# Cross attention on one Trainium2 core: the reads of the stacked low key halves are issued from ScalarE's queue

## The reference

```
x = x + tanh(g_xattn) * attention(layernorm(x), ctx, ctx)    # 16 heads of 16, q from x, k and v from ctx
x = x + tanh(g_ffn)   * ffn(layernorm(x))                    # gated experts into v, attention, gated experts out

# cross attention, 32 batches, 100 queries, 361 keys, width 256
scores = (q @ k.T) / sqrt(16);  scores = where(mask, scores, min);  attn = softmax(scores)
O = (attn @ v) @ Wo.T + bo
```

## Time and profile before

| | |
|---|---|
| median of 3 runs | 2054.14 us (2052.46 to 2054.36) |
| the profiled execution: time | 2055.4 us |
| the profiled execution: span | 2053.6 us |
| busy in the span | PE 93%, DVE 73%, ACT 56%, POOL 45% |
| issues of line 405 | 256 of 90.2 KB, median 4.9 us from issue to landing |

### The profile page before, as it was taken

One profiled execution on the slowest core, in us unless ns is written; L12 is line 12 of the kernel. 1 busy time (PEld: TensorE's weight loads), 2 busy tenths in 40 slices (PEclk: granted clock), 3 DMA queues, 4 the chain that ended last, 5 costly groups with the idle time before them and its releaser, 6 DMA issues. The chain is left out here.

```text
span 2053.6 us, 59326 instructions
## 1 busy us (share of the span) xinstructions
PE 1916.2 (93%) x13454; PEld 1163.7 (57%) x13454; DVE 1497.0 (73%) x4285; ACT 1143.3 (56%) x3588; POOL 933.5 (45%) x1361
## 2 busy tenths in 40 slices
PE   5698999999988799999999999968999999999998
PEld 2477777777777555544444444436555555555553
DVE  6477777777777796255555555555999999999989
ACT  3477777777777644444444444434555555555543
POOL 3011121122111200266666666653766666777767
PEclk9899999999999899999999999987999999999999
DMA  3666665676666158300000000025222222222201
GB/s 115 114 106 97 103 108 99 104 102 105 106 101 89 51 223 322 128 26 26 26 26 26 26 26 26 26 91 165 79 73 76 72 76 72 76 75 70 84 14 64
DMA packets 192129, 173.99 MB, mean 85 GB/s; under 512 B 51921, under 2 KB 183378, under 8 KB 190034
## 3 DMA queue, kind: packets, MB, share of 16 engines
q1 hardware_dynamic: 189906, 165.06, 34.5%
q0 software_dynamic: 2176, 8.39, 1.2%
HBM read 112.41 MB, written 60.98 MB: 84 GB/s over the span
## 5 line engine op out<-in xcount | busy, mean ns | idle before, releaser
L1315 POOL TENSOR_TENSOR o_side<-o_side,o_tmp 128x256 f32 (+1 forms) x528 | 397.7, 753 | 192.2 <-POOL o_side L1315 73.2
L593 ACT ACTIVATE c_ex<-c_sm,c_nmax 100x361 f32<-100x361 f32 x512 | 303.9, 594 | 157.7 <-DVE c_nmax L486 136.5
L1041 ACT ACTIVATE big<-e_pv,gates 128x128 f32<-128x128 f32 x800 | 228.7, 368 | 291.4 <-PE e_pv L1103 290.1
L486 DVE CUSTOM_DVE_ANT_0 c_sm<-c_ps,c_mbias 100x361 f32<-100x361 f32 x512 | 270.3, 528 | 137.7 <-PE c_ps L665 135.8
L1436 ACT ACTIVATE o_tmp<-o_py,gates 128x256 f32<-128x256 f32 x528 | 222.3, 474 | 190.6 <-PE o_py L1509 140.8
L1103 PE MATMUL e_pv<-e_vhi,e_xhi 128*128 x800 | 303.2, 379 | 1.2 <-ACT e_out L1031 1.2
L1509 PE MATMUL o_py<-o_whi,a_chi 128*128 128x512 f16 x800 | 303.9, 380 | 0.1
L979 DVE TENSOR_SCALAR e_acc<-e_pv,gates 128x128 f32<-128x128 f32 x400 | 122.0, 347 | 249.1 <-PE e_pv L1103 249.1
L1103 PE MATMUL e_pv<-e_vlo,e_xhi 128*128 x800 | 303.2, 379 | 0.0
L1103 PE MATMUL e_pv<-e_vhi,e_xlo 128*128 x800 | 303.2, 379 | 0.0
L1509 PE MATMUL o_py<-o_wlo,a_chi 128*128 128x512 f16 x800 | 303.2, 379 | 0.0
(11 more groups left out here) (166 smaller groups left out, 3397.4 us busy)
## 6 DMA issues: line engine op xcount, KB each, us to landing
qk<-e_out SPq DMA_DIRECT2D x16, 1600.0 KB, 5.2
c_kst<-k_parts SPq DMA_DIRECT2D x256, 90.2 KB, 4.9
v<-e_out SPq DMA_DIRECT2D x20, 640.0 KB, 3.3
a_q<-qk SPq DMA_DIRECT2D x64, 200.0 KB, 2.4
a_k<-qk SPq DMA_DIRECT2D x64, 200.0 KB, 2.5
a_v<-v SPq DMA_DIRECT2D x64, 200.0 KB
c_ctx<-in_ctx_t SPq DMA_DIRECT2D x32, 361.0 KB, 3.2
e_wst<-in_v_w POOLq DMA_DIRECT2D x8, 1024.0 KB, 6.7
```

Of the source, the lines that this page charges most:

```text
L486: dve.tensor_tensor_reduce(out=sm[:, h % 4, :], in0=p_s[0:SQ, h % 2, 0:SK], in1=mbias[:, b.par, :], scale=-0.25 / WS, scalar=BIG, op0=ALU. ...
L593: act.activation(ex[:, h % 4, 0:SK], sm[:, h % 4, :], ACT.Exp, scale=-1.0, bias=nmax[:, h % 4:h % 4 + 1], accum_out=den[:, b.par, HEAD[h]: ...
L1041: act.activation(tmp[:, hh, e, :], p_v[:, hh, 1, e * PD:(e + 1) * PD], ACT.Copy, scale=gate).then_inc(s_av, 1)
L1315: pool.tensor_tensor(side[:, x.t, :], side[:, x.t, :], tmp[:, slot(x, r), j, :], ALU.add).then_inc(s_pool, 1)
```

## The change

A helper `stack_part` issues the four reads of one half. SyncE calls it for the high half at the old place. ScalarE calls it for the low half: once after the values of batch 0, and then in step 11 of each batch but the last, after that step's exponential, with the two waits that SyncE had (all scores of the batch before the current one computed, and the write of the low half landed). Sources, destinations, sizes and semaphores of the transfers are the same.

```diff
+        def stack_part(eng, b, part, landed):
+            eng.wait_ge(landed[b.par], 16 * (b.half + 1))
+            src = k_parts[b.par, part, :, :].rearrange("(j a d) s -> a d j s", a=2, d=XD)
+            for ab in range(2):
+                for r in (part, part + 2):
+                    row = 64 * ab + XD * r
+                    eng.dma_start(kst[row:row + XD, b.par, :, :], src[ab]).then_inc(s_kst[b.par], 16)
...
                     at_least(sp, s_s, XH * (b.n - 1))
-                    for part, landed in enumerate((s_kwh, s_kwl)):
-                        sp.wait_ge(landed[b.par], 16 * (b.half + 1))
-                        src = k_parts[b.par, part, :, :].rearrange("(j a d) s -> a d j s", a=2, d=XD)
-                        for ab in range(2):
-                            for r in (part, part + 2):
-                                row = 64 * ab + XD * r
-                                sp.dma_start(kst[row:row + XD, b.par, :, :], src[ab]
-                                             ).then_inc(s_kst[b.par], 16)
+                    stack_part(sp, b, 0, s_kwh)
...
                 for c in range(KC):
                     values(fixed(0), c)
+                stack_part(act, fixed(0), 1, s_kwl)
...
                         if i in (8, 10, 14) and not is_last(b):
                             values(b.next(), (8, 10, 14).index(i))
+                        if i == 11 and not is_last(b):
+                            at_least(act, s_s, XH * b.n)
+                            stack_part(act, b.next(), 1, s_kwl)
```

## The result

The changed kernel takes 2105.22 us (median of 4 runs, 2103.13 to 2107.74) against 2054.25 us (2052.46 to 2060.39). The ratio is 1.0228, 95% interval 1.0205 to 1.0250: slower, as forecast, but by 51 us and not by 91. The profiled execution took 2105.4 us, with a span of 2103.6.

The account below looks back on a forecast made before the run. The last `kst` landing was taken to bound each of 31 cross-attention boundaries. 2.0 + 0.3 us per boundary gave 71 us, the clock 20 us; added to 2055.4 us: 2146 us, range 2122 to 2170 us.

Parts of the forecast that it names:

- What bounds the kernel: At 31 cross-attention boundaries, the landing of the last of eight `kst` reads starts the next batch; TensorE waits 23.6 us.
- SyncE's four issues: Freeing SyncE of four issues of 0.43 us starts nothing there earlier: gain 0.
- The time of the issue: ScalarE's first low-half issue comes 0.5 us after the start of step 11's exponential, between 0.1 and 0.9.
- The duration of the burst: The low half's four reads take 6.2 us from first issue to fourth landing; fastest 4.4 us from the exponential.
- The neighbours: Small `qst` reads on SyncE's queue, running beside the low half, cost 0.3 us per boundary, between 0 and 1.0.
- The reference boundary: One boundary, at 366.85 us, gave 4.66 us from step 11's exponential to the next batch, the base for all 31.
- ScalarE's issues cost 0 in step 11: Four issues hold ScalarE 1.7 us and delay `turn` from 365.70 to 366.3, covered by the late keys: cost 0.
- The signs of being wrong: Exponential-to-batch distance under 5 us, TensorE's wait before step 0 not ending on `kst`, or step 11's exponential moving against batch start.
- The clock: Longer TensorE idling at boundaries adds 15 slow-clock stretches of 1.3 us each to the cross attention: 20 us.
- The early issue with an unchanged clock: Rival: issue at 0.1 us, small reads free, no added slow stretch; 51 us more, 2106 us; chance 0.19.
- A hidden move: Rival: low-half reads on their own queue land quicker, 4.7 us from the exponential; time stays 2055 us; chance 0.04.
- a faster kernel: Rival: issue at 0.1 us, landing at 4.5 us; boundary wait shrinks, slow stretches go; 2038 us; chance 0.03.

Follow-up runs that it names:

- Experiment 2: Changed kernel with ScalarE's four low-half issues in step 9 instead of step 11: 2066.90 us, ratio 1.0036 to the kernel before.
- experiment 3: Changed kernel with ScalarE's four low-half issues in step 13 instead of step 11: 2215.62 us, ratio 1.0762 to the kernel before.
- Experiment 4: Changed kernel without the small `qst` reads from batch 2 on, using the queries of batches 0 and 1: 2110.75 us, ratio 1.0245 to the kernel before.
- experiment 7: Changed kernel with two of the four low reads back on SyncE, two on ScalarE in step 11: 2054.13 us, ratio 0.9985 to the kernel before.
- experiment 1: Changed kernel with all eight reads on SyncE, the last four waiting for step 10's exponential: 2091.39 us, ratio 1.0159 to the kernel before.
- experiments 5 and 6: Idle TensorE matmuls around the boundary, added to the kernel before (6 and 5): 2041.98 us; to the changed kernel (6 and 14): 2063.62 us.

## Why the prediction came out as it did

**What bounds the kernel: right.** The last landing of `kst` set each of the 31 boundaries before and after. Experiment 2 shows the other side: with the keys in early, the next wait (ScalarE's copy) takes over.

**SyncE's four issues: 0, right.** SyncE gained nothing from being freed: the reads of `qst` go out 3.09 us behind the exponential of step 11 (364.65), before 3.07 (365.26).

**The time of the issue: mis-sized.** I took 0.5 us behind the start of the exponential, between 0.1 and 0.9. It is 0.24 us ahead of it, outside both ends. The bound "0.1" assumed that the issue follows the exponential's start; but the stream had passed it while the copy of head 7 was still at work. The Trainium skill (Perfetto Trace Analysis, Per-engine timelines) has the sequencer push an instruction and go on; the trace agrees here (361.32 against 361.56). It doesn't where the exponential itself has to wait for VectorE: in experiment 3, after 1.17 us of idle time, the first issue comes 0.01 to 0.09 us behind the exponential's start at all 31 boundaries.

**The duration of the burst: mis-sized.** I took 6.2 us from first issue to fourth landing, from the old burst's first four; it is 5.7 (361.32 to 367.0), and 5.64 in the mean of the 30 batches. The first four of the old burst take 6.33 in the mean. A part of the difference came from the reads behind them: the high half of the changed kernel, with no low half behind it, takes 6.08. The other 0.44 us stay. The high half still runs while the write of the low half is on its way (issued 356.62, landed 359.4), in both kernels; that this slows it is an argument and was not tried. The bound from the fastest landing, 4.4 us, was too low.

**The neighbours: 0.3 taken, not measured apart.** Experiment 4 put other transfers in their place. Whatever they cost is inside the 5.7 us of the burst, for which the sum had 6.2 + 0.3. With the -0.24 and the 5.7 the forecast of this boundary falls by 0.74 + 0.8, from 6.96 to about 5.4 us; the first scores follow the landing by 0.2, and 5.65 were measured.

**The reference boundary.** 4.66 us was one boundary. The mean of the 30, worked out from the same kind of rows, is 4.85 before and 5.52 after. So of the term of 2.3 us per boundary 0.7 to 0.8 were left (71 us forecast, 20 to 24 measured). This is the step that failed, by its size: the late issue and the burst behind it were both priced too high.

**ScalarE's issues cost 0 in step 11: right, but not for the reason given.** I had them delay `turn` by 0.6 us and the late keys cover that. `turn` was not delayed at all (3.50 us behind the exponential, before 3.51): the issues start earlier than I took, and the idle time ahead of step 13, which I had left out, takes up the rest. Experiment 2 shows them where that cover is missing: about 1.3 us more waiting for ScalarE's copies per batch.

**The signs of being wrong** did not appear: the distance stays over 5 us from the second boundary on, TensorE's wait ends on `kst`, and at full clock the exponential of step 11 has not moved against the batch's start (13.44 us, before 13.46).

**The clock: right in kind, close in size.** 15 additional slow stretches and 20 us were forecast; there are 18, and they cost 23 to 27 us, half of the whole loss or a little more. The forecast of 2146 us was too high because of the other term alone.

**The rivals.** The early issue with an unchanged clock gave 2106 us, by chance nearly the measured time: its issue was the nearest (0.1 us behind, against 0.24 ahead), but its distance grew by 1.6 us instead of 0.7, and it had no slow stretch added instead of 18. A hidden move and a faster kernel fell; experiment 7 shows what a hidden move would have needed, no gap on the DMA engines.

**Left open:** what makes the low half's burst 0.44 us quicker than the high half's in the same kernel, what the small reads of `qst` cost it, and the 2.0 us behind the last boundary.

## What to carry to other kernels

A transfer that is last at a boundary is priced by when its burst leaves a gap on the DMA engines, not by which queue issues it: two reads could be moved behind the backlog for nothing, four left a gap and cost 0.7 to 0.8 us each time. Where TensorE waits at such a boundary, a wait that grows by less than a microsecond can double its price through the clock, and idle matmuls in the gap get that part back, in the kernel before as well (0.7%). Issues put into a compute engine's stream take their place in its order: look for the step where that engine has idle time behind it.

## What the runs showed of the hardware

A transfer issued by ScalarE doesn't wait for the end of the ACTIVATE in front of it. Where that one only stood behind a running copy, the first issue came 0.23 to 0.26 us ahead of its start; where it waited for VectorE (experiment 3), just behind its start, by 0.09 us at most. The ACTIVATEs behind the issues wait for them: 0.32 to 0.45 us each, 1.77 us for four (361.32 to 363.09), and the next exponential follows 0.17 us later. The granted clock follows small idle times of TensorE around the boundary. Ahead of the last `turn` of a batch it is idle for about 0.6 us in the kernel before and in the changed one alike. The wait behind that `turn`, for the keys, is 0.76 us in the mean before (23.6 in 31), 1.19 in experiment 1 (37.0 in 31) and 1.42 in the changed kernel (44.1 in 31), and 9, 25 and 27 of 30 batches have a slow stretch. The length of this wait alone doesn't decide it: in the kernel before one of 0.79 us was followed by a slow stretch and one of 0.94 us was not. A single wait of 1.40 us elsewhere in the batch (experiment 2) went with only 3. With the idle time filled by matmuls (experiments 5 and 6) there are none. And more idle time (experiment 3, 1.98 and 3.23 us) made the slow stretches longer, with a mean clock of 0.86 instead of 0.92.
